# Start-up of a two-layer conditioned block: weight loads in steps, set-up rows on other engines, and three orders changed

## The reference

```python
def ada(x, gw, bw): return (t @ gw.T)[:, None] * rmsnorm(x) + (t @ bw.T)[:, None]
a = attention(ada(x, attn_gamma_w, attn_beta_w))        # 16 heads of 16, softmax, W_q W_k W_v W_o
x = x + (t @ attn_alpha_w.T)[:, None] * a
h = ada(x, ffn_gamma_w, ffn_beta_w)
f = (silu(h @ gate_w.T) * (h @ hidden_w.T)) @ out_w.T + out_b      # 1024 hidden
x = x + (t @ ffn_alpha_w.T)[:, None] * f
y = (layernorm(x) * weight + bias + tanh(t @ lin_w.T + lin_b)[:, None]) * weight + bias
```

## Time and profile before

| What | Value |
|---|---|
| Median of three runs | 490.44 us |
| The profiled execution | 493.41 us, span 491.6 us |
| TensorE busy | 474.5 us, 97% of the span |
| VectorE, ScalarE, GpSimd busy | 76%, 49%, 56% |
| Granted TensorE clock, mean | 0.983 |
| Chain that ended last | TensorE 89%, VectorE 3%, GpSimd 2%, ScalarE 2%, DMA 2% |

### The profile page before, as it was taken

The page is one execution under the profiler, slowest core; times in us unless marked ns, Lnnn a source line. Parts: engine busy times, 40 slices in busy tenths (PEclk is TensorE's granted clock), DMA queues, the critical chain, the costliest instruction groups (busy, mean ns, idle before and its releaser), DMA issues.

```text
span 491.6 us, 11925 instructions
## 1 busy us (share of the span) xinstructions
PE 474.5 (97%) x4547; PEld 402.7 (82%) x4547; DVE 373.2 (76%) x770; ACT 241.7 (49%) x373; POOL 273.4 (56%) x192
## 2 busy tenths in 40 slices
PE   7799999999999999999999999999999999999992
PEld 4677778898879987898888988798888988889992
DVE  5869776578877789777886788777896688774765
ACT  3765754246452655427462554536553375413341
POOL 3464655644577543855468445774538554626673
PEclk9959999999999999999999999999999999999997
DMA  8761086301822044500944027420645007400113
GB/s 198 249 169 48 1 212 150 54 2 40 219 71 83 1 141 116 139 10 0 230 65 110 0 76 180 107 43 0 171 97 138 0 11 162 127 4 1 44 47 82
DMA packets 36044, 44.23 MB, mean 90 GB/s; under 512 B 3120, under 2 KB 31024, under 8 KB 36016
## 3 DMA queue, kind: packets, MB, share of 16 engines
q1 hardware_dynamic: 36016, 43.85, 35.7%
HBM read 35.18 MB, written 4.47 MB: 81 GB/s over the span
## 4 chain that ended last, share of the span: by engine, by line
PE 89%; DVE 3%; POOL 2%; ACT 2%; DMA 2%; issue 1%; DVEq 0%; SPq 0%; POOLq 0%
PE banks L767 31%; PE banks L785 17%; PE banks L510 7%; PE banks L616 6%; PE banks L806 5%; PE banks L700 4%; PE banks L545 4%; PE banks L659 3%; PE banks L664 3%; PE banks L822 2%; PE banks L604 2%; PE banks L581 2%; DMA x2g<-woT_in 2%; PE banks L467 1%; PE banks L737 1%
## 5 line engine op out<-in xcount | busy, mean ns | idle before, releaser
L767 PE MATMUL banks<-x2s,gh 128*128 128x512 f32 x672 | 167.5, 397 | 0.7 <-ACT x2s L1088 0.5
L767 PEld LDWEIGHTS banks<-x2s,gh 128*128 128x128 f32 x672 | 122.7, 188 | 28.1 <-issue 0.9
L1787 POOL TENSOR_TENSOR hs<-act_t,hs 128x512 fp32r<-128x512 f32 x56 | 72.0, 1286 | 126.5 <-ACT hs L1050 99.8
L785 PE MATMUL banks<-wout,hs 128*128 128x256 f32 x672 | 91.6, 285 | 0.5 <-POOL hs L1787 0.5
L785 PEld LDWEIGHTS banks<-wout,hs 128*128 128x128 f32 x672 | 85.3, 188 | 5.3 <-POOL hs L1787 0.7
L1050 ACT ACTIVATE hs<-act_t 128x512 fp32r<-128x512 f32 x56 | 35.3, 630 | 70.7 <-DVE act_t L1461 70.6
L1043 ACT ACTIVATE act_t<-banks 128x512 f32<-128x512 f32 x56 | 33.5, 598 | 68.7 <-PE banks L767 68.2
L1457 DVE SCALAR_TENSOR_TENSOR act_t<-act_t,banks 128x512 f32<-128x512 f32 x56 | 38.4, 685 | 31.2 <-ACT act_t L1043 30.8
L1371 DVE RECIPROCAL work_c<-banks 128x512 f32<-128x512 f32 x14 | 47.0, 3355 | 3.3 <-PE banks L659 3.3
L510 PE MATMUL banks<-xs,wqk 128*128 128x512 f32 x192 | 47.6, 394 | 0.7 <-ACT xs L978 0.7
L1461 DVE SCALAR_TENSOR_TENSOR act_t<-act_t,banks 128x512 f32<-128x512 f32 x56 | 38.5, 687 | 5.1 <-PE banks L767 2.0
(11 more groups left out here) (158 smaller groups left out, 748.9 us busy)
## 6 DMA issues: line engine op xcount, KB each, us to landing
xtok<-x_in SPq DMA_DIRECT2D x8, 512.0 KB, 5.1
work_c<-xn SPq DMA_DIRECT2D x16, 256.0 KB, 3.5
row_aa<-rows_dram SPq DMA_DIRECT2D x16, 256.0 KB, 6.9
xres<-x_in SPq DMA_DIRECT2D x8, 512.0 KB, 7.2
row_af<-rows_dram SPq DMA_DIRECT2D x16, 256.0 KB, 7.4
row_b<-rows_dram SPq DMA_DIRECT2D x16, 256.0 KB, 6.1
shift<-rows_dram SPq DMA_DIRECT2D x16, 256.0 KB, 6.0
y<-final SPq DMA_DIRECT2D x7, 512.0 KB, 3.2
```

The source lines that it names most:

```text
L767: last = mm(banks[:, base + part, :], gh[:, a, k, w:w + P], x2s[:, b, k, :], start=(n == 0), stop=(n == 5))
L785: last = mm(banks[:, t // 2, D * (t % 2):D * (t % 2) + D], hs[:, c % 2, b, P * t:P * t + P], wout[:, a, c, :], start=(c == 0 and a == b an ...
L1787: tt(hs[:, c % 2, 1, :], act_t[:, c % 2, :], hs[:, c % 2, 0, :].bitcast(F32), ALU.subtract)\
```

## The change

Five things change, all ahead of group 1's main part:

- SP waits for piece 2 before it asks for pieces 3 and 4, and for piece 3 before 5 and 6.
- ScalarE spreads the selectors first of all, copies three set-up rows out of PSUM, and copies k (`pair_k`) before it rounds `wo` (`cut_hi(2)`). Its tanh moves behind `place_v_kept(0)`.
- The sums and products of the set-up rows go from VectorE to GpSimd (`join_rows`, ahead of `cut_lo(2)`), and GpSimd's `finish_shift` moves behind `cut_lo(4)`. VectorE loses six small operations.
- Group 0's v is projected in two halves, the second behind the first `scores_for_max`.
- In the head of group 1 the first half of q moves behind the transposes of x2, and there is one warm-up where there were three.

```diff
             load_stage(2)
+            sp.wait_ge(ld_stage[2], 16)
             load_stage(3)
             load_stage(4)
+            sp.wait_ge(ld_stage[3], 16)
             load_stage(5)
             load_stage(6)
-            sp.wait_ge(setup_dve, SETUP_ALPHAS)
+            sp.wait_ge(rows_copied, SETUP_COPIES)
+            sp.wait_ge(rows_joined, 2)
...
-WARM_LOADS, WARM_LAST_MAX, WARM_MAX, WARM_NORM = 3, 2, 2, 3
+WARM_LOADS, WARM_LAST_MAX, WARM_MAX, WARM_NORM = 3, 2, 2, 1
...
                 elif not later(g):
-                    pe.wait_ge(tables_ready, 3)
+                    pe.wait_ge(tables_ready, 2)
+                    pe.wait_ge(rows_copied, SETUP_COPIES)
                 project_qk(g, 0, bank_of_q(g), q_mm)
...
-                project_v(base, range(V_EARLY if later(g) else TT))
+                if later(g):
+                    project_v(base, range(V_EARLY), v_mm)
+                else:
+                    project_v(base, range(2))
...
                 else:
-                    project_qk(g, 0, bank_of_q(g), q_mm, (0,))
                     transpose_x2(g - 1)
-                    project_qk(g, 0, bank_of_q(g), q_mm, (1,))
+                    q_proj(g)
                     pe.wait_ge(k_ready, 4 * g + 4)
                     warm_up(wqk[:, 0, 0], WARM_NORM, bank_of_k(g))
...
                 scores_for_max(0, 0)
+                project_v(bank_of_v(0), (2, 3), v_mm)
                 scores_for_max(0, 1)
...
+            def copy_rows():
+                act.wait_ge(rows_mm, 1)
+                nc.scalar.activation(cvec, banks[0:B, 2, 0:D], ACT.Copy).then_inc(rows_copied, 1)
+                nc.scalar.activation(rows[:, R_AA, :], banks[0:B, 2, D:2 * D], ACT.Copy).then_inc(rows_copied, 1)
+                act.wait_ge(tables_ready, 2)
+                nc.scalar.activation(rows[:, R_AF, :], banks[0:B, TABLE_BANK[OTHER_TABLES], D:2 * D], ACT.Copy)\
+                    .then_inc(rows_copied, 1)
...
             def first():
+                setup_selectors()
                 cut_hi(0)
                 cut_hi(1)
                 setup_identity()
                 x0_split()
-                nc.scalar.activation(sel[:, :, :].rearrange("p c (e k) -> p (c e) k", e=2),
...
-                act.wait_ge(setup_dve, SETUP_TANH)
-                nc.scalar.activation(cvec, cvec, ACT.Tanh).then_inc(setup_act, 1)
+                copy_rows()
+                pair_k(0, range(2))
                 cut_hi(2)
-                pair_k(0, range(2))
                 cut_hi(3)
                 pair_q(0)
...
                 place_v_kept(0)
+                act.wait_ge(rows_joined, 1)
+                nc.scalar.activation(cvec, cvec, ACT.Tanh).then_inc(setup_act, 1)
                 cut_hi(4)
...
+            def join_rows():
+
+                pool.wait_ge(ld_lin, LD_SHIFT)
+                pool.wait_ge(rows_copied, SETUP_COPIES)
+                tt(cvec, cvec, linb_b[0:B], ALU.add).then_inc(rows_joined, 1)
+                tt(rows[:, R_B, :], rows[:, R_AF, :], outb_b[0:B], ALU.mult).then_inc(rows_joined, 1)
+                tt(w2[:, :], lnw_b, lnw_b, ALU.mult).then_inc(rows_joined, 1)
...
+                join_rows()
                 cut_lo(2)
                 cut_lo(3)
+                cut_lo(4)
                 finish_shift()
-                cut_lo(4)
                 cut_lo(5)
                 xs_split(1)
```

More of the change, by code:

```diff
@@ L52 @@
 LD_SHIFT = 16 * 4
-SETUP_TANH, SETUP_ALPHAS, SETUP_SHIFT = 1, 4, 3
-WARM_LOADS, WARM_LAST_MAX, WARM_MAX, WARM_NORM = 3, 2, 2, 3
+SETUP_COPIES, SETUP_SHIFT = 3, 3
+WARM_LOADS, WARM_LAST_MAX, WARM_MAX, WARM_NORM = 3, 2, 2, 1
 BLOCKS = 2 * CH
@@ L172, in build @@
         zeroed, selectors_ready = sem("zeroed"), sem("selectors_ready")
-        tables_mm, rows_mm, tables_ready, identb_ready, setup_dve, setup_act, setup_pool = map(
-            sem, ("tables_mm", "rows_mm", "tables_ready", "identb_ready", "setup_dve", "setup_act", "setup_pool"))
+        tables_mm, rows_mm, tables_ready, identb_ready, rows_copied, rows_joined, setup_act, setup_pool = map(
+            sem, ("tables_mm", "rows_mm", "tables_ready", "identb_ready", "rows_copied", "rows_joined", "setup_act", "setup_pool"))
         stage_hi, stage_lo = sem("stage_hi"), sem("stage_lo")
@@ L539, in v_proj, with project_v @@
                     pe.wait_ge(x2_steps, X2)
-                project_v(base, range(V_EARLY if later(g) else TT))
-            def project_v(base, tiles):
+                if later(g):
+                    project_v(base, range(V_EARLY), v_mm)
+                else:
+                    project_v(base, range(2))
+            def project_v(base, tiles, done=None):
                 for t in tiles:
@@ L546, in project_v @@
                                   xs[:, a, k, P * t:P * t + P], wv[:, b, k, :], start=(n == 0), stop=(n == 5))
-                last.then_inc(v_mm, 1)
+                if done is not None:
+                    last.then_inc(done, 1)
             def v_rest(g):
@@ L554, in v_rest @@
                     pe.wait_ge(v_out, 2)
-                project_v(-(V_EARLY // 2), range(V_EARLY, TT))
+                project_v(-(V_EARLY // 2), range(V_EARLY, TT), v_mm)
             def scores_for_max(g, n):
@@ L967, in cut_hi, with setup_selectors @@
                 nc.scalar.activation(chunks[n][1], stage_view(n), ACT.Copy).then_inc(stage_hi, 1)
+            def setup_selectors():
+                act.wait_ge(ld_tables, LD_TABLE)
+                nc.scalar.activation(sel[:, :, :].rearrange("p c (e k) -> p (c e) k", e=2),
+                                     cst[:, C_SEL:C_SEL + 2 * G * SEQ].unsqueeze(2).to_broadcast([P, 2 * G * SEQ, L]),
+                                     ACT.Copy).then_inc(selectors_ready, 1)
+            def copy_rows():
[5 more added lines that the diff above has]
+                    .then_inc(rows_copied, 1)
             def setup_identity():
@@ L1123, in first @@
                 x0_split()
-                nc.scalar.activation(sel[:, :, :].rearrange("p c (e k) -> p (c e) k", e=2),
-                                     cst[:, C_SEL:C_SEL + 2 * G * SEQ].unsqueeze(2).to_broadcast([P, 2 * G * SEQ, L]),
-                                     ACT.Copy).then_inc(selectors_ready, 1)
-                act.wait_ge(setup_dve, SETUP_TANH)
-                nc.scalar.activation(cvec, cvec, ACT.Tanh).then_inc(setup_act, 1)
+                copy_rows()
+                pair_k(0, range(2))
                 cut_hi(2)
-                pair_k(0, range(2))
                 cut_hi(3)
@@ L1273, in setup_tables @@
                               banks[:, TABLE_BANK[names], 0:len(names) * KD * B]).then_inc(tables_ready, 1)
[L1274 to L1286, removed]
             def square_sum(x, scratch, total, done):
@@ L1552, in first @@
             def first():
-                setup_rows()
-                setup_weights()
                 dve.wait_ge(stage_lo, 1)
```

## The result

| | before | after |
|---|---|---|
| Median of 20 executions | 490.50 us (489.28 to 493.38) | 491.93 us (490.36 to 494.40) |
| The profiled execution | 493.41 us, span 491.6 | 494.15 us, span 492.4 |
| Granted TensorE clock, mean | 0.983 | 0.985 |

The ratio is 1.003, 95% interval 1.0016 to 1.0045: 0.8 to 2.2 us slower, under the 0.5% that the prediction called measurable. It had 491.0 and "same". Both profiled executions are slow ones of their kernel: 494.15 is the second slowest of the 20 after, and 493.41 lies above all 20 of before. So what the two profiles differ by need not be what the medians differ by.

The account below looks back on a forecast made before the run. TensorE was taken to bound everything after start-up, so only the first 56 us could move. From the profiled 493.4, -2.0 (clock up, GpSimd stopping the chain) and -0.3 (group 1's head) made 491.1, forecast as 491.0; range 488.0 to 493.5.

Parts of the forecast that it names:

- Sum: Whole kernel: before's median has no or less clock fall than its profile; 491.1 with clock up, +0.6 against that median.
- rival D: TensorE's clock: before's median did contain the fall and the change removes it; 488.1, or 487.6; chance 0.13.
- Part 1: Weight loads in steps: `wo` gains nothing, piece 3 lands at 21.4 against 19.2.
- let it stay at 18.0: Landing of `wo`: late from work ahead of it, not behind; taken to gain nothing, bounds nothing or 3.5 us.
- rival C: Load on the queues made `wo` late; x and `wo` land 3.5 us earlier; 488.6; chance 0.15.
- Part 2: ScalarE's order: k's copies earlier, but piece 3's rounding makes the first maximum +0.85 late; selectors hidden, tanh +0.42.
- Part 3: VectorE and GpSimd: `cut_lo(5)` ends at 37.4 and GpSimd stops the chain to 39.8 against 41.86, -2.0.
- Worth nothing: VectorE's six lost operations, about 2 us before 16: no gain, as it then waits for the second x.
- Part 4: v split: 1.5 us of v fills the hole before the second scores; worth nothing by itself at one clock.
- clock up: TensorE's clock doesn't fall after 24: first exponential at 31.7 against 33.57, kernel 491.1 on the profile's basis.
- Part 5: Head of group 1, second q behind x2's transposes, fewer warm-ups: between -0.15 and -0.6, taken as -0.3.
- Rival B: TensorE's clock falls in the changed kernel too, to 0.50 after 25; slower, 494.0; chance 0.17.

Follow-up runs that it names:

- refilled kernels: Changed kernel with VectorE's first memset done ten times: ratio to before 1.0008; with weight piece 7 also later 0.9992; then without SP's two waits 0.9969.
- piece 7 later: Weight piece 7 asked for only after VectorE's fourth product: 0.9995 in the changed kernel, 0.9983 in the kernel before, 0.9992 in the changed kernel with VectorE's nine extra instructions.

## Why the prediction held, and where it didn't

**The reading of the median of before** (Sum) was right. Beside the refilled kernels before ran 29 times: the four with a mean clock of 0.983 took 493.3 to 494.1, those at 0.989 and above 489.6 to 491.6. So the median has no long fall, rival D had nothing to win, and the 3 us between profile and median were the clock.

**Part 1.** The step "let it stay at 18.0" failed. `wo` landed at 15.9, 5.7 after its request; over the nine kernels with the waits it took 5.6 to 6.7, over the four without 6.2 to 7.6. So by the prediction's own sign (`wo` before 16.5) this was rival C, and its mechanism was there, but at about 1 us on average (6.0 against 7.1) instead of 3.5, and its 488.6 did not come. Part of what the pair of profiles shows is spread. The rule of ring order (the Trainium skill, "DMA: Bandwidth & Descriptors", section "Queues, rings and completion order") would give 0 by itself. The two groups overlap, but three of the four without the waits took longer than all nine with them. The transfer of piece 3 was sized well (3.8 against 3.4 to 4.1), only asked for two microseconds earlier than I had it, so it landed at 19.7 and not at 21.4, and the first maximum ran at 23.70 and not at 25.0. The direction was right: the steps delay piece 3. ScalarE's wait on it is hidden in the changed kernel's profile only because k came at half clock (23 matmuls in 7.00 against 5.54) and was later still.

**Part 2.** The selectors cost nothing (7.04 to 8.96) and the tanh 0.42, as said. k's copies ahead of `wo` took effect.

**Part 3.** GpSimd's `cut_lo(5)` ended at 37.08 against a forecast of 37.4 (its terms add up to 37.3), with the remainder of xs right behind it, to 39.40 against 39.8. The stop it makes is real, and shows once nothing else is slower. "Worth nothing" for VectorE's lost instructions failed at a place that I didn't look at: the last store, 0.8 us in the profiles. The prediction said it would be wrong if something outside the first 56 us changed, and there it was.

**Part 4.** The split does no work and wins none at one clock, as costed; undoing it left the ratio where it was (1.0031). Whether it holds the clock up is only suggested by single executions: between 24 and 35 the clock fell in the profiles of all four kernels with v whole, and in three of nine with v split. The case "clock up" held in this execution. The first exponential came at 30.68, forecast 31.7; the first maximum was 1.3 early and 0.3 went between it and the exponential.

**Part 5.** From the first residual to gate: 10.66 after, 10.86 with the old order, 10.87 in before with the waits. That is -0.2, inside -0.15 to -0.6, and too little for the medians. Over all profiles the four with the old order have 10.86 to 11.26 and the nine with the new one 10.65 to 11.20, so the size is no better known than that.

**What was missing** was the price of arriving early. Up to the exponentials the change is 2.9 ahead of the profile of before and 0.9 ahead of the kernel with the old order of q, whose clock fell to 0.80 in 24 to 28. Then it stops for 2.09 where that one stops for 1.12, as the block of instructions begins at nearly the same time in both (37.33 and 37.20), and behind the stop comes a fall that costs 1.5. It reaches the residual 1.6 later. For an execution like the profiled one, with the clock up in 24 to 35, the forecast was 491.1, and it took 494.15. The sum's +0.6 against the median and the measured +1.4 lie close because terms offset that the prediction did not have: piece 3 earlier than costed, against the stop, the fall and the store. To that extent the hit is luck. How many of the other 19 executions had the stop and the fall no trace shows. From the medians, each in its own comparison: the change +1.43 over before; with VectorE refilled +0.40; with piece 7 later as well -0.22; without the waits too -1.32. Every step of that line is about the size of its own uncertainty (0.7 to 1 us); only its two ends are measured apart from 0, and the last step is in part the clock. And the last is not clearly better than the kernel before with piece 7 later, -1.05: of the change proper, nothing measurable remains.

Rival B's fall did not come at 25; one came at 40, behind the stop.

## What to carry to other kernels

Before costing a gain in start-up, look for what is bound to a time and not to the chain: instruction blocks on the queue list, and large loads that can be asked for later. A wait between two loads helps the first only by what the profile shows it shared, and it delays the second by a whole landing; ask who needs the second. Instructions removed from an engine can move an instruction block onto something that counts, even where their work was hidden.

## What the runs showed of the hardware

- **A block of TensorE's instructions can be late.** In the profiles of the seven kernels with the stop TensorE went on 2.48 to 2.58 us behind the start of a 16 KB block. The Trainium skill, "Runtime: NRT & Kernel Launch", section "Instruction fetch mechanics", says that instructions are refilled in blocks of 16 KiB and that the cost is mostly hidden. The size of the blocks on q8 agrees; here up to 2.5 us were not hidden.
- **A stop can be followed by a fall of the clock or not.** Stops of 0.60, 1.08, 1.12, 1.82 and 1.94 us were followed by a clock of 1.00 in 40 to 44, those of 2.09 and 2.50 by 0.57 in the same stretch. These are single executions.
- **An 8 KB instruction block on q14 beside the last store of 128 KB** made its landing 2.8 us instead of 2.0 (after against before). With nine instructions added to VectorE the last block on q14 began at 484.52 and the landing was 2.0 again.
- **The clock falls at other places in other executions**: 0.64 in 12 to 16 after, 1.00 there in before. Single profiles differ by more than the change is worth.
